# A clamp and a scaling of state ends, moved from GpSimd into VectorE's carry instruction

## The chip, the cores and the metric

The kernel runs on one core of a Trainium2 chip. The metric is the device time in microseconds (us) of one execution, median over the runs. Engines are named as the profile names them: PE is TensorE's matmul, PEld its weight load, DVE is VectorE, ACT is ScalarE, POOL is GpSimd, SP is SyncE. SBUF and PSUM are the two on-chip memories; in this kernel the tiles PM, PAZ and YB lie in PSUM, all other tiles in SBUF.

## What is computed

The reference is a block of a state-space model followed by a mixture of experts. Input x is 8 batches x 1024 steps x 256, inner width 512, state size 16. The part that matters here is the recurrence over time and its clip at every tenth step:

```python
def step(h, inp):
    dA_t, dB_t, x_t, C_t, t = inp
    h = h * dA_t + dB_t * x_t[:, :, None]
    nrm = jnp.sqrt(jnp.sum(h * h, axis=(1, 2), keepdims=True))
    fac = jnp.minimum(20.0 / (nrm + 1e-08), 1.0)
    h = jnp.where(t % 10 == 0, h * fac, h)
    y = jnp.einsum('bdn,bn->bd', h, C_t) + D_param * x_t
    return (h, y)
```

So the states run freely for ten steps, then the whole state of a batch (512 x 16 numbers) is scaled by one factor of at most 1. Behind it come the gate, the output projection, a residual and a layer norm, then a router that takes the best 2 of 8 experts with a capacity, the two expert matmuls, and a second layer norm.

## The kernel before, in words

**Two phases.** `ssm_phase` does the recurrence and its surroundings, `moe_phase` the experts. The change touches only the first, which takes the first 33 or so of the 40 slices of the span. It is a software pipeline over 52 blocks of 20 steps (index i); each block has 16 slots s, the same for each engine. A slot belongs to one batch and one chunk: a block is four quarters (r = s // 4, q = 4 i + r), each the chunk of 10 steps for 4 of the 8 batches, and u = s % 4 is the batch in it. Each engine has its own program with the same two loops, and the order of its work is written out by hand: what stands under which s runs in that order, and semaphores (`wait_ge`, `then_inc`) join the engines.

**The recurrence on VectorE.** For each slot a multiply (`mult`, L579) writes the inputs dB x for 64 rows x 10 steps into PSUM, and a scan (`scan`, L610) runs 64 rows x 11 columns (704 elements per partition), of which column 0 of each row holds the state that is carried in: the decay there is 0, so the scan starts each row from it. The scan writes H, of which three buffers exist (q % 3). Column 10 of each row is the end state. For every two slots one `carry` (L584 to L596) puts the carried states, 2 batches x 64 rows, into column 0 of the scan's input: for q of 2 and more it copies them from the tile CAR. So there are two carries in each q, at u = 0 and u = 2, 412 in all beside four memsets for the first two q. Within two slots VectorE's order is mult(u), carry(u), mult(u + 1), at u = 2 a sum of the norm (L617), the product U = dt x (L566) in two of the 16 slots, scan(u), and then scan(u + 1); at u = 0 the gated output of an earlier q (L631) stands between the two scans. Four further instructions of the block stand between scans and carries: XC (L647, s = 6, ahead of the carry), VV (L697, s = 13), the statistics of a layer norm (L656, s = 14, ahead of the carry; L665 behind it), SG (L705, s = 15) with LGS (L714).

**The clip.** ScalarE squares the end states of q - 1 (L398, one instruction of 256 elements, rows 11 elements apart), TensorE sums them over the partitions (L862), VectorE over the rest (L617, into SN). GpSimd, at u = 2 of q (p = q - 1), raises the sum to the power of -0.5 (L755), multiplies by 1.25 and limits to 1 (L757), and multiplies the end states of p by this factor into CAR (L760), for which it first waits until the carries of p + 1 have read CAR's earlier contents. Carry(q + 1) reads CAR a quarter later: the clip's factor applies to the states that enter chunk p + 2, which is the same batches' next chunk.

**GpSimd's other work.** In every slot it multiplies the ten columns of H by C (L775, 640 elements, in place, "HC" below), which waits for the scan of the slot; TensorE then sums over the 16 states (L820). Besides, per block: L726 (s = 8), L730 (s = 10), L737 and L743 (s = 14), L750 (s = 1), L780 to L786 (s = 3), L793 and L797 (s = 7), in the order in which they stand in the code.

Of the kernel before, what the change touches and what calls it, by code (L numbers as in the profile page):

```python
# [8 lines left out]
ALU = mybir.AluOpType  # L9
ACT = mybir.ActivationFunctionType  # L10
# [12 lines left out]
def ok(j):  # L23
    return 0 <= j < NB
# [77 lines left out]
def ssm_phase(nc, d, YA, X2d, LGd, Bd, Cd, RB, IOE):  # L102
    ctx = ExitStack()
    with ctx:
        def sb(name, shape, dt=F32):
            return ctx.enter_context(nc.sbuf_tensor(name, shape, dt))

        def sem(name):
            return ctx.enter_context(nc.semaphore(name))

        DA = sb("DA", [128, 4, 8, 4, 16, 11])
        H = sb("H", [128, 3, 4, CH])
# [38 lines left out]
        SQ = sb("SQ", [128, 4, 64])  # L151
        SN = sb("SN", [128, 2, 4])
        HALF = sb("HALF", [128, 4])
        FC = sb("FC", [128, 2, 4])
        CAR = sb("CAR", [128, 4, 64])
        PM = ctx.enter_context(nc.psum_tensor("PM", [128, 2048], F32))

        PAZ = ctx.enter_context(nc.psum_tensor("PAZ", [128, 1024], F32))
# [15 lines left out]
        s_bcs, s_ln, s_dth, s_tg, s_z64, s_da, s_x2t, s_hsq = (  # L174
            sem("bcs"), sem("sp"), sem("dth"), sem("tg"), sem("z64"), sem("da"), sem("x2t"), sem("hsq"))

        s_halo, s_sgh, s_dx, s_dxh, s_hc, s_slot = sem("halo"), sem("sgh"), sem("dx"), sem("dxh"), sem("hc"), sem("slot")
        s_min, s_dt, s_xn, s_pow, s_fac, s_car = (
            sem("min"), sem("dt"), sem("xn"), sem("pow"), sem("fac"), sem("car"))
        s_ve, s_sd, s_x2 = sem("ve"), sem("sd"), sem("x2")  # L180

        s_br, s_ssum, s_cv, s_gt, s_dtp = sem("br"), sem("ssum"), sem("cv"), sem("gt"), sem("dtp")
# [2 lines left out]
        s_xc, s_u, s_sg, s_m1, s_ca, s_scan, s_red = (  # L185
            sem("xc"), sem("u"), sem("sg"), sem("m1"), sem("ca"), sem("scan"), sem("red"))
# [19 lines left out]
        def cols(c):  # L206
            return 11 if c < NC - 1 else 1 + (L - 1) % 10
# [5 lines left out]

        def decays(c, g):
            return DA[:, c % 4, 4 * g:4 * g + 4].rearrange("p b a n t -> p b (a n t)")[:, :, 0:64 * cols(c)]

        def U(c):
            return PM[:, 320 * (c % 2):320 * (c % 2) + 320].rearrange("p (a b t) -> p a b t", a=4, b=8)
# [142 lines left out]
        def scalar_program(eng):  # L361
# [11 lines left out]
            def exp_a(j, n):  # L373

                c = 2 * j + n // 2
                v = decays(c, n % 2).rearrange("p b (a t) -> p b a t", t=cols(c))[:, :, :, 1:cols(c)]
                eng.activation(v, v, ACT.Exp, scale=16.0).then_inc(s_da, 1)  # L377
# [12 lines left out]
            for i in range(-4, NB + 3):  # L390
                for s in range(16):
                    q = 4 * i + s // 4
                    if s % 4 == 0 and 1 <= q <= NQ - 2:

                        eng.wait_ge(s_scan, 4 * q)
                        if q >= 2:
                            eng.wait_ge(s_nrm, q - 1)
                        eng.activation(SQ[:], H[:, (q - 1) % 3].rearrange(  # L398
                            "p u (a t) -> p u a t", t=11)[:, :, :, 10], ACT.Square).then_inc(s_hsq, 1)
                    if s == 0 and ok(i + 3):  # L400

                        j = i + 3
# [91 lines left out]
                    if s == 14 and ok(i + 1):  # L494
                        j = i + 1
                        eng.wait_ge(s_gt, 2 * (j + 1))
                        if ok(i + 2):
                            eng.wait_ge(s_xc, j + 2)
                        eng.activation(TB[:].rearrange("p (m a) b t -> p m (a b t)", m=2), BOTH, ACT.Tanh,
                                       scale=0.5).then_inc(s_tg, 1)  # L500
                    if ok(i + 1):
                        j = i + 1
                        c0 = (2 * j) % 4
                        for n in range(DUE[s], DUE[s + 1]):
                            a, m = n // 16, n % 16
                            if n == 0:
# [10 lines left out]
                                scale=AS[:, a, m:m + 1]).then_inc(s_z64, 1)  # L517
# [9 lines left out]
        def vector_program(eng):  # L527
# [56 lines left out]
            def carry(q, u):  # L584

                k = cols(q // 2)
                o = PM[:, 640:640 + 2 * CH].rearrange("p (u n) -> p u n", u=2)[:, :, 0:64 * k].rearrange(
                    "p u (a t) -> p u a t", t=k)[:, :, :, 0]
                if 4 * q + u >= 2:
                    eng.wait_ge(s_scan, 4 * q + u)  # L590
                if q < 2:
                    eng.memset(o, 0.0).then_inc(s_ca, 1)
                else:
                    if u == 0:
                        eng.wait_ge(s_car, q - 1)
                    eng.tensor_copy(o, CAR[:, u:u + 2]).then_inc(s_ca, 1)  # L596

            def scan(q, u):
                eng.wait_ge(s_m1, 4 * q + u + 1)
                eng.wait_ge(s_ca, 2 * q + u // 2 + 1)  # L600
                c, g = q // 2, q % 2
                if u == 0:
                    if q >= 2:
                        eng.wait_ge(s_da, q - 1)
                    if c == NC - 1:
                        eng.wait_ge(s_slot, 1)
                    if q >= 3:
                        eng.wait_ge(s_ys, 3 * (q - 2))
                n = 64 * cols(c)
                eng.tensor_tensor_scan(H[:, q % 3, u, 0:n], decays(c, g)[:, u], DBX(u)[:, 0:n], 0.0, ALU.mult,  # L610
                                       ALU.add).then_inc(s_scan, 1)
# [22 lines left out]
            for i in range(-4, NB + 3):  # L634
                live = ok(i)
                for s in range(16):
                    r, u = s // 4, s % 4
                    q = 4 * i + r
# [18 lines left out]
                    if live and u % 2 == 0:  # L657
                        carry(q, u)
                        mult(q, u + 1)
# [56 lines left out]
        def gpsimd_program(eng):  # L716
            eng.wait_ge(s_pre, PRE_CV)
            for i in range(-4, NB + 3):
                live = ok(i)
                for s in range(16):  # L720
                    r, u = s // 4, s % 4
                    q = 4 * i + r
# [28 lines left out]
                    if u == 2 and 1 <= q <= NQ - 2:  # L751

                        p = q - 1
                        eng.wait_ge(s_red, p + 1)
                        eng.tensor_tensor(FC[:, p % 2], SN[:, p % 2], HALF[:], ALU.pow).then_inc(s_pow, 1)  # L755
                        eng.wait_ge(s_pow, p + 1)
                        eng.tensor_scalar(FC[:, p % 2], FC[:, p % 2], 1.25, 1.0, ALU.mult, ALU.min).then_inc(s_fac, 1)  # L757
                        eng.wait_ge(s_fac, p + 1)
                        eng.wait_ge(s_ca, 2 * (p + 2))
                        eng.tensor_tensor(CAR[:], H[:, p % 3].rearrange("p u (a t) -> p u a t", t=11)[:, :, :, 10],  # L760
                                          FC[:, p % 2].unsqueeze(2).to_broadcast([128, 4, 64]),
                                          ALU.mult).then_inc(s_car, 1)
                    if i == NB - 2 and s == 0:

                        k = cols(NC - 1)
# [177 lines left out]
        with nc.Block() as block:  # L943
            @block.sync
            def _(eng):
                sync_program(eng)

            @block.scalar
            def _(eng):
                scalar_program(eng)  # L950

            @block.vector
            def _(eng):
                vector_program(eng)

            @block.gpsimd
            def _(eng):
                gpsimd_program(eng)

            @block.tensor  # L960
            def _(eng):
                tensor_program(eng)
# [423 lines left out]
def build(nc, d, out):  # L1386
    YA = nc.dram_tensor("YA", [B * LP, DM], F32, kind="Internal").ap()
    X2d = nc.dram_tensor("X2d", [B * LP, DM], F32, kind="Internal").ap()
    LGd = nc.dram_tensor("LGd", [128, 8 * B, E], F32, kind="Internal").ap()
    Bd = nc.dram_tensor("Bd", [NC, 2, NS, 40], F32, kind="Internal").ap()  # L1390
    Cd = nc.dram_tensor("Cd", [NC, 2, NS, 40], F32, kind="Internal").ap()
    with ExitStack() as ctx:
        RB = ctx.enter_context(nc.sbuf_tensor("RB", [128, 4096], F32))
        IOE = ctx.enter_context(nc.sbuf_tensor("IOE", [128, 8], F32))
        ssm_phase(nc, d, YA, X2d, LGd, Bd, Cd, RB[:], IOE[:])
        moe_phase(nc, d, YA, X2d, LGd, out, RB[:])
# [43 lines left out]
```

## Time and profile before

| what | value |
|---|---|
| time, median of 3 runs | 2773.16 us (2772.2 to 2776.47) |
| profiled execution, its span | 2772.7 us (no other time is given for it) |
| busy share of the span | PE 94%, PEld 86%, DVE 86%, ACT 81%, POOL 77% |
| DVE in the 40 slices, tenths | 2999999999999999999999999999999997221124 |
| POOL in the 40 slices, tenths | 0789888898888988989889889898898883434314 |
| granted TensorE clock in the slices | 9899999999999999999999999999999987999996 |
| span on core 0, mean granted clock | 2772.7 us, 0.975 |

A slice is 69.3 us. Each digit is the share of the slice in which the engine was busy, in tenths, where 9 is 90% or more. The recurrence fills slices 2 to 33; the experts follow.

In the rows below, times are us from the start of the span unless marked ns. In a timeline the first number is the start, the second the duration of the record. Records of VectorE follow each other closer than their durations say (the next starts some 0.08 us before the last one's end), so the time that an instruction takes of the engine is read from one start to the next. "x2" means that two instructions in a row are merged into one line.

### The profile page before, as it was taken

What the parts mean: (1) busy time and instruction counts of PE and PEld (TensorE: products, weight loads), DVE (VectorE), ACT (ScalarE), POOL (GpSimd) and SP (SyncE); (2) the same over time, 40 slices, a digit from 0 to 9 for tenths busy, and PEclk for the clock granted to TensorE, in tenths of its full rate; (3) what the DMA queues carried; (4) which work ended last, traced back from release to release, by engine and by line L of the source; (5) the groups of instructions that cost most, each with busy time, mean ns of one, the idle gap of its engine ahead of it and who ended that gap; (6) DMA issues with size and microseconds to landing.
All of it is one profiled execution on the core that took longest, in us unless ns stands there. A gap on an engine that the chain in (4) does not pass through costs nothing. (4 is left out here: it accounts for less than half of the span.)

```text
span 2772.7 us, 50775 instructions
## 1 busy us (share of the span) xinstructions
PE 2593.0 (94%) x16812; PEld 2388.8 (86%) x16812; DVE 2382.4 (86%) x3391; ACT 2245.1 (81%) x5074; POOL 2134.4 (77%) x2237
## 2 busy tenths in 40 slices
PE   5899999999999999999999999999999986899992
PEld 4899999999999999999999999999999975677762
DVE  2999999999999999999999999999999997221124
ACT  5999999999999999999999999999999962111113
POOL 0789888898898988989889889898898883434314
PEclk9899999999999999999999999999999987999996
DMA  1222222222222222222222222222222222234227
GB/s 61 70 78 78 79 80 78 78 78 81 77 78 75 80 79 78 78 78 82 78 78 78 81 78 78 76 78 80 78 78 78 75 78 93 48 93 105 61 48 254
DMA packets 145746, 225.65 MB, mean 81 GB/s; under 512 B 37836, under 2 KB 84684, under 8 KB 144332
## 3 DMA queue, kind: packets, MB, share of 16 engines
q1 hardware_dynamic: 123044, 188.95, 22.4%
q0 software_dynamic: 9216, 12.59, 2.6%
q10 hardware_dynamic: 13224, 20.86, 2.2%
q8 instruction: 134, 2.20, 0.3%
q14 instruction: 128, 1.05, 0.1%
HBM read 189.27 MB, written 33.05 MB: 80 GB/s over the span
## 5 line engine op out<-in xcount | busy, mean ns | idle before, releaser
L775 POOL TENSOR_TENSOR H<-H,CB 128x640 f32<-128x640 f32 (+1 forms) x832 | 1216.2, 1476 | 157.1 <-DVE H L610 154.9
L610 DVE TENSOR_TENSOR_SCAN H<-DA,PM 128x704 f32<-128x704 f32 (+1 forms) x832 | 1309.4, 1594 | 0.0
L514 ACT ACTIVATE DA<-DT,SM 128x160 f32<-128x160 f32 (+1 forms) x3328 | 1106.8, 421 | 1.6 <-POOL DT L737 0.3
L820 PE MATMUL YB<-H,ID 128*128 128x160 f32 (+1 forms) x6656 | 1043.9, 309 | 0.2 <-POOL H L775 0.2
L820 PEld LDWEIGHTS YB<-H,ID 128*128 128x128 f32 x6656 | 982.3, 191 | 16.4 <-issue 11.2
L579 DVE TENSOR_TENSOR PM<-PM,BB 128x640 f32<-128x640 f32 (+1 forms) x832 | 673.1, 809 | 0.0
L377 ACT ACTIVATE DA<-DA 128x2560 f32<-128x2560 f32 (+1 forms) x206 | 477.7, 2319 | 1.7
L755 POOL TENSOR_TENSOR FC<-SN,HALF 128x4 f32<-128x4 f32 x206 | 232.8, 1130 | 40.8 <-DVE SN L617 36.8
L826 PE MATMUL PAZ<-XN,RB 128*128 128x160 f32 x1664 | 254.7, 307 | 0.1
L836 PEld LDWEIGHTS PAZ<-XB,CD 128*128 128x128 f32 x1664 | 237.5, 188 | 16.8
L845 PE MATMUL PAZ<-XC,RB 128*128 128x160 f32 x1664 | 244.4, 300 | 3.3 <-DVE XC L647 3.3
L1285 POOL DMA_INDIRECT YA<-YS,IG x48 | 75.1, 1566 | 219.8 <-ACT YS L1116 208.2
L836 PE MATMUL PAZ<-XB,CD 128*128 128x160 f32 x1664 | 243.1, 297 | 0.0
L826 PEld LDWEIGHTS PAZ<-XN,RB 128*128 128x128 f32 x1664 | 237.9, 195 | 0.7 <-ACT CS L467 0.3
L845 PEld LDWEIGHTS PAZ<-XC,RB 128*128 128x128 f32 x1664 | 231.1, 190 | 6.4 <-DVE XC L647 4.0
L921 PE MATMUL PAZ<-WO,Z 128*80 128x256 f32 x832 | 189.1, 380 | 0.0
L862 PE MATMUL YB<-SQ,MEAN 128*128 128x128 f32 x824 | 131.3, 282 | 43.0 <-ACT SQ L398 43.0
L760 POOL TENSOR_TENSOR CAR<-H,FC 128x256 f32<-128x256 f32 x206 | 155.4, 754 | 17.3
L921 PEld LDWEIGHTS PAZ<-WO,Z 128*80 128x80 f32 x832 | 125.3, 151 | 49.4 <-issue 0.7
L1359 PE MATMUL PE<-W,HT 128*128 128x256 f32 x768 | 167.2, 379 | 0.8 <-issue 0.8
L1348 PE MATMUL PE<-XTE,W 128*128 128x384 f32 x512 | 167.3, 488 | 0.0
L1359 PEld LDWEIGHTS PE<-W,HT 128*128 128x128 f32 x768 | 145.3, 190 | 20.8 <-issue 1.3
(157 smaller groups left out, 2779.7 us busy)
## 6 DMA issues: line engine op xcount, KB each, us to landing
BB<-Bd SPq DMA_DIRECT2D x208, 320.0 KB, 3.4
CB<-Cd SPq DMA_DIRECT2D x208, 320.0 KB, 3.2
W<-in_w ACTq DMA_DIRECT2D x16, 1024.0 KB, 7.9
XT<-in_xT SPq DMA_DIRECT2D x52, 160.0 KB, 2.2
XR<-in_xp SPq DMA_DIRECT2D x208, 40.0 KB
X2d<-VV SPq DMA_DIRECT2D x208, 40.0 KB
YA<-VV SPq DMA_DIRECT2D x208, 40.0 KB
HI<-YA SPq DMA_DIRECT2D x6, 1024.0 KB, 9.9
```

The source lines that it names most:

```text
L377: eng.activation(v, v, ACT.Exp, scale=16.0).then_inc(s_da, 1)
L514: eng.activation(DA[:, c0 + k0:c0 + k1, :, a, m, 1:11].rearrange("p c b t -> p b c t"), DT[:, j % 2, a].rearrange("p b (c t) -> p b c t", ...
L579: eng.tensor_tensor(DBX(u)[:, 0:64 * k].rearrange("p (a n t) -> p a n t", a=4, n=16)[:, :, :, 1:k], U(c)[:, :, 4 * g + u, 0:k - 1].unsquee ...
L610: eng.tensor_tensor_scan(H[:, q % 3, u, 0:n], decays(c, g)[:, u], DBX(u)[:, 0:n], 0.0, ALU.mult, ALU.add).then_inc(s_scan, 1)
L755: eng.tensor_tensor(FC[:, p % 2], SN[:, p % 2], HALF[:], ALU.pow).then_inc(s_pow, 1)
L775: eng.tensor_tensor(h, h, cb, ALU.mult).then_inc(s_hc, 1)
L820: mm = eng.matmul(yv, ID[:], hv[:, :, :, n, 0:w], start=False, stop=n == 15)
L826: mm = eng.matmul(p[:, 160 * a:160 * a + 160], WIN[:, k, c0 + 128 * a:c0 + 128 * a + 128], XN[:, j % 2, k], start=k == 0, stop=k == 1)
L836: mm = eng.matmul(p[:, 160 * a:160 * a + 160].rearrange("p (b t) -> p b t", b=8), CD[:, k, 2 * m + a], XB[:, 2 * m + a, :, k:k + 20], star ...
L845: mm = eng.matmul(p[:, 160 * a:160 * a + 160], WDT[:, k, c:c + 128], XC[:, j % 2, k].rearrange("p b t -> p (b t)"), start=k == 0, stop=k == 3)
L921: mm = eng.matmul(PZ[0:80, 256 * g:256 * g + 256], zf[:, a, 80 * g:80 * g + 80], WO[:, a, :], start=a == 0, stop=a == 3)
L1359: t = eng.matmul(bank(n)[:, 256 * h:256 * h + 256], HT[:, m, 128 * (2 * c + h):128 * (2 * c + h) + 128], W2[:, e % 2, m, :], start=m == 0, ...
```

## The change

The tile CAR and the semaphores `s_fac` and `s_car` go. GpSimd keeps only the power. The factor 1.25 moves into ScalarE's square, which now takes 0.8 h, so that the power yields 1.25 divided by the norm measure. The limit to 1 and the multiplication by the end states are done by VectorE's carry, which was a copy and is now one `scalar_tensor_tensor`: it takes the factor from FC (one number per partition and batch, read with step 0 over 64 rows), the minimum with 1, and multiplies by the end states, read directly from H with a step of 11 elements. It waits for the power (`s_pow`) where it waited for CAR. GpSimd's power waits until the carries of p, which read the FC buffer before, are done.

```diff
-        CAR = sb("CAR", [128, 4, 64])
...
+        def ends(q):
+            return H[:, q % 3].rearrange("p u (a t) -> p u a t", t=11)[:, :, :, 10]
...
-                        eng.activation(SQ[:], H[:, (q - 1) % 3].rearrange(
-                            "p u (a t) -> p u a t", t=11)[:, :, :, 10], ACT.Square).then_inc(s_hsq, 1)
+                        eng.activation(SQ[:], ends(q - 1), ACT.Square, scale=0.8).then_inc(s_hsq, 1)
...
                     if u == 0:
-                        eng.wait_ge(s_car, q - 1)
-                    eng.tensor_copy(o, CAR[:, u:u + 2]).then_inc(s_ca, 1)
+                        eng.wait_ge(s_pow, q - 1)
+                    eng.scalar_tensor_tensor(
+                        o, FC[:, q % 2, u:u + 2].unsqueeze(2).to_broadcast([128, 2, 64]), 1.0, ends(q - 2)[:, u:u + 2],
+                        ALU.min, ALU.mult).then_inc(s_ca, 1)
...
                         eng.wait_ge(s_red, p + 1)
+                        if p >= 2:
+                            eng.wait_ge(s_ca, 2 * (p + 1))
                         eng.tensor_tensor(FC[:, p % 2], SN[:, p % 2], HALF[:], ALU.pow).then_inc(s_pow, 1)
-                        eng.wait_ge(s_pow, p + 1)
-                        eng.tensor_scalar(FC[:, p % 2], FC[:, p % 2], 1.25, 1.0, ALU.mult, ALU.min).then_inc(s_fac, 1)
-                        eng.wait_ge(s_fac, p + 1)
-                        eng.wait_ge(s_ca, 2 * (p + 2))
-                        eng.tensor_tensor(CAR[:], H[:, p % 3].rearrange("p u (a t) -> p u a t", t=11)[:, :, :, 10],
-                                          FC[:, p % 2].unsqueeze(2).to_broadcast([128, 4, 64]),
-                                          ALU.mult).then_inc(s_car, 1)
```

## Rows read from the trace of the kernel before

**Rows 1.** Windows by stretch: us and instructions of each engine, clock, DMA share, GB/s

```profile
1000.00:1500.00 500.00, 491.28 (x3400) 466.89 (x3400) 500.00 (x679) 480.00 (x1065) 442.11 (x464) 1.00 0.27 78
...
102.00:144.00 42.00, 38.52 (x249) 37.26 (x248) 40.25 (x52) 38.00 (x83) 34.91 (x35) 0.92 0.22 67
```

**Rows 2.** VectorE's groups by form, whole span: busy us, mean ns, idle before

```profile
L596 DVE COPY PM<-CAR 128x128 f32<-128x128 f32 x412 | 115.3, 280 | 1.6 <-POOL CAR L760 1.6
...
L566 DVE TENSOR_TENSOR PM<-DT,XC 128x320 f32<-128x320 f32 x104 | 51.8, 498 | 0.0
...
L1225 DVE TENSOR_TENSOR YS<-PE,B 128x512 f32<-128x512 f32 x24 | 16.6, 691 | 147.4 <-PE PE L1359 147.4
...
L549 DVE MEMSET DA<- 128x1536 f32 x1 | 1.3, 1338 | 1.4 <-issue 1.4
...
L86 DVE TENSOR_TENSOR RB<-RB 128x448 f32<-128x448 f32 x2 | 1.5, 752 | 0.1
...
L1153 DVE TENSOR_TENSOR POS<-PE,CI 128x512 f32<-128x512 f32 x1 | 1.0, 1016 | 0.0
```

**Rows 3.** GpSimd's groups by form, whole span

```profile
L775 POOL TENSOR_TENSOR H<-H,CB 128x640 f32<-128x640 f32 x824 | 1210.5, 1483 | 154.1 <-DVE H L610 152.0
L755 POOL TENSOR_TENSOR FC<-SN,HALF 128x4 f32<-128x4 f32 x206 | 232.8, 1130 | 40.8 <-DVE SN L617 36.8
L760 POOL TENSOR_TENSOR CAR<-H,FC 128x256 f32<-128x256 f32 x206 | 155.4, 754 | 17.3
...
L757 POOL TENSOR_SCALAR FC<-FC 128x4 f32<-128x4 f32 x206 | 47.9, 232 | 18.5
```

**Rows 4.** Timeline of VectorE, 1000 to 1045 us: start, us, instruction

```profile
1004.44 0.80 DVE L579 TENSOR_TENSOR PM<-PM,BB 128x640 f32<-128x640 f32 x1
1005.16 0.28 DVE L596 COPY PM<-CAR 128x128 f32<-128x128 f32 x1
1005.35 0.82 DVE L579 TENSOR_TENSOR PM<-PM,BB 128x640 f32<-128x640 f32 x1
...
1007.82 1.60 DVE L610 TENSOR_TENSOR_SCAN H<-DA,PM 128x704 f32<-128x704 f32 x1
1009.35 0.66 DVE L697 SCALAR_TENSOR_TENSOR VV<-XR,PAZ 80x512 f32<-80x512 f32 x1
...
1011.32 0.27 DVE L596 COPY PM<-CAR 128x128 f32<-128x128 f32 x1
...
1031.51 0.80 DVE L579 TENSOR_TENSOR PM<-PM,BB 128x640 f32<-128x640 f32 x1
...
1032.95 0.28 DVE L596 COPY PM<-CAR 128x128 f32<-128x128 f32 x1
```

**Rows 5.** Timeline of GpSimd, 1000 to 1045 us

```profile
1009.51 1.49 POOL L775 TENSOR_TENSOR H<-H,CB 128x640 f32<-128x640 f32 x1 [0.20 <-DVE H L610]
1011.08 0.72 POOL L737 TENSOR_SCALAR DT<-TA 128x640 f32<-128x640 f32 x1
```

**Rows 6.** Timeline of VectorE, 2225 to 2310 us

```profile
2234.31 0.97 DVE L566 TENSOR_TENSOR PM<-DT,XC 128x320 f32<-128x320 f32 x1
2235.20 3.12 DVE L610 TENSOR_TENSOR_SCAN H<-DA,PM 128x704 f32<-128x704 f32 x2
...
2307.39 0.88 DVE L86 TENSOR_TENSOR RB<-RB 128x448 f32<-128x448 f32 x1
```

**Rows 7.** Timeline of GpSimd, 2225 to 2310 us

```profile
2232.02 2.91 POOL L775 TENSOR_TENSOR H<-H,CB 128x640 f32<-128x640 f32 x2
2234.89 1.25 POOL L755 TENSOR_TENSOR FC<-SN,HALF 128x4 f32<-128x4 f32 x1
...
2306.70 1.09 POOL L786 TENSOR_SCALAR VV<-VV,NME,SD 80x256 f32<-80x256 f32 x2
```

**Rows 8.** ScalarE's groups by form, whole span

```profile
L398 ACT ACTIVATE SQ<-H 128x256 f32<-128x256 f32 x206 | 134.1, 651 | 8.7 <-DVE H L610 8.6
...
L408 ACT ACTIVATE TB<-XT 128x320 f32<-128x320 f32 x52 | 23.7, 456 | 0.0
```

More of the change, by code:

```diff
@@ L177, in ssm_phase @@
         s_halo, s_sgh, s_dx, s_dxh, s_hc, s_slot = sem("halo"), sem("sgh"), sem("dx"), sem("dxh"), sem("hc"), sem("slot")
-        s_min, s_dt, s_xn, s_pow, s_fac, s_car = (
-            sem("min"), sem("dt"), sem("xn"), sem("pow"), sem("fac"), sem("car"))
+        s_min, s_dt, s_xn, s_pow = sem("min"), sem("dt"), sem("xn"), sem("pow")
         s_ve, s_sd, s_x2 = sem("ve"), sem("sd"), sem("x2")
```

## The prediction

> **What bounds the kernel now.** I read the profile's page first, for the phases: its slices show VectorE at 9 tenths through the recurrence. Then the windows inside that phase, then the groups by form of the three engines that the change touches, and last VectorE's and GpSimd's timelines side by side. In the window of 500 us VectorE is busy for all 500.00, TensorE 491.28, ScalarE 480.00, GpSimd 442.11 [rows 1]. VectorE has no gap, so each nanosecond added to one of its instructions here lengthens the loop, and each one taken from GpSimd is worth nothing unless VectorE waits for GpSimd. It does so once in the whole trace, for 1.6 us ahead of a carry [rows 2]; GpSimd waits for VectorE's scans, for 152 us in all [rows 3].
>
> **What the change removes.** GpSimd loses 206 instructions of 232 ns and 206 of 754 ns [rows 3], some 203 us of busy time and a little idle time between them. It lies beside VectorE's work and shortens nothing. The 1.6 us may go: the power was ready far earlier than CAR. I count -1.6 us. ScalarE's square gets a constant scale instead of none: the same instruction of 651 ns [rows 8], on an engine with 4% of slack; nothing. Should it cost 50 ns, four a block are 0.2 us, and the slack of a block is over 1 us. GpSimd's new wait, for the carries of p, is always met: by then VectorE has gone past the carries of p + 1. The tile and the two semaphores cost no time. No DMA is moved, and no queue of SP or GpSimd is passed.
>
> **What it adds.** VectorE's 412 copies become 412 instructions with two inputs, FC and H, both in SBUF. A copy takes 0.19 us from its start to the next one's, 1005.16 to 1005.35 [rows 4]. Three prices are to be found.
>
> First, the pure work. The copy of 128 elements is 280 ns, a two-input operation of 512 elements with one input in PSUM is 691 ns [rows 2]; the line through both is 1.07 ns per element on 143 ns. At 320 elements it gives 485; L566, which has both inputs in SBUF, has 498 on average, and without its one long instance (970) it is 493 [rows 2, 6]. So a second input costs nothing by itself, and I take 0.
>
> Second, the step of 11 elements in H. No VectorE instruction before reads SBUF so. The nearest is L1153, which reads CI with a step of 64 elements (and PSUM with the same): 1016 ns against 691 for L1225 at the same 512 elements [rows 2], 0.63 ns per element, so 0.081 us for 128 and 33.4 us for 412. The low end is 0: L549 writes every eleventh element and takes 1338 ns for 1536, 0.87 ns each [rows 2]. A gain is excluded, since the same number of elements is read. The high end is ScalarE, which reads these very end states: 651 ns for 256 against 456 for 320 contiguous ones [rows 8]; with 64 elements less counted at 1.07 ns that is 263 ns too much, 1.03 each, 0.132 us for 128 and 54 us for 412. I take 33.4, from the row of the same engine.
>
> Third, and largest, GpSimd. Two places show what VectorE does when both inputs are in SBUF and GpSimd is in the middle of an instruction. L566 at 2234.31 lasts 0.97 us in place of 0.49 [rows 6, 2], while GpSimd's two HC run to 2232.02 + 2.91 = 2234.93 [rows 7]: it was lengthened by 0.48, which is the 0.62 us to GpSimd's end less 0.14. The following scan starts at 2235.20, so the engine lost it in full. L86 at 2307.39 lasts 0.88, where its two instances sum to 1.5 us, so the other had 0.62 [rows 6, 2]; GpSimd's L786 runs to 2306.70 + 1.09 = 2307.79 [rows 7]: 0.40 to its end, 0.26 too long, again 0.14 less. The other 103 L566 stand right behind the norm sum, where GpSimd waits for that sum, and meet nothing. Scans, mults and the copy have at most one input in SBUF and keep their durations beside HC all along.
>
> The Trainium skill's page "SBUF — State Buffer", section "Who interferes with whom", has the rule: a VectorE instruction with two SBUF inputs and a GpSimd instruction that reads SBUF share a read interface, and whichever comes second is blocked until the first is done. By that rule, the trace agrees. The Trainium skill's page "Advanced Engine Details and Errata", section "SBUF Cachelines", says that accesses which each go to another 16-byte line pay a penalty, but gives no price; by it the zero end of the second price falls away, while the memset's row shows no penalty.
>
> Where does GpSimd stand when a carry asks? Call T the start of VectorE's first instruction behind the second scan of a pair (1009.35). GpSimd's HC of that scan starts at 1009.51 = T + 0.16 and ends 1.49 later, at T + 1.65 [rows 4, 5]. The carry asks one mult behind T: 1005.16 - 1004.44 = 0.72 [rows 4]. So it finds HC running and waits 1.65 - 0.72 - 0.14 = 0.79 us. With two instructions gone GpSimd is less loaded than now, so each such HC starts when its scan ends; its block of extra work falls behind HC and is over before the next pair. Of the eight carries of a block five are like this (s = 2, 4, 8, 10, 12): 3.95 us. At s = 6 XC stands ahead, and the carry asks at T + 1.44, 1031.51 to 1032.95 [rows 4]: 0.07. At s = 0 SG and LGS stand ahead: 0. At s = 14 VV and the statistics stand ahead, and the carry at 1011.32 meets DT, which runs 1011.08 to 1011.80 [rows 4, 5]: 0.34. Sum 4.36 us a block; 412 / 8 = 51.5 blocks make 224.5 us. Low end: waits of 0, if FC's step-0 read did not count as an SBUF input. High end: no 0.14 to be deducted, six times 0.14 x 51.5 = 43 more.
>
> **The sum.** 2772.7 + 224.5 + 33.4 - 1.6 = 3029.0 us for the profiled execution; the median of the runs shown is 0.5 above its span, within their spread, so I forecast 3029. TensorE, at 98% of the loop now, falls to some 88% and ScalarE to 86%; neither hides any of this, for VectorE is late in every slot. Late next is GpSimd's HC, by the same amount, then TensorE's sums.
>
> **Rivals.**
> *A, the engines slide past each other.* If HC and carries meet at random, the mean wait is the sum of squared durations over twice the block: 16 x 1.483² + 4 x 1.13² is 40, over 94 gives 0.43, less 0.14 x 28/47 is 0.35 us. 412 x 0.35 = 144, so 2772.7 + 144 + 33 - 2 = 2948. For it: GpSimd's extra work moves HC; against it: HC is tied to the scan and the carry too. 11%.
> *B, not slower.* VectorE gets its operands at once, because a factor of two numbers a partition is hardly a stream, and the strided read is free as the strided memset was. Place: each carry; it decides if carries stay at 0.2 us from start to start. Then 1.6 us are gained, and 0.48 at the one long L566: 2770.6, less than 0.1% below. Against it: L566 and L86. 3%, with 1 more for a gain over 0.2%, for which no row has a source.
> *C, only the stride costs:* 2772.7 + 33.4 - 1.6 = 2804.5. 4%.
> *D, GpSimd goes twice.* If its next ready instruction enters ahead of the waiting carry, slots 4, 8 and 10 wait for L780, L793 or L730 too; at the 0.72 us of L737 [rows 5] for each that is 2.2 us a block, 111 in all: 3140. Against it: L755 was ready at 2234.89 and was itself stretched, to 1.25 us [rows 7], so VectorE came first. 3%.
> *E, TensorE's clock.* The granted clock is 1.00 at 98% busy and 0.92 in the stretch where TensorE was busy for 38.52 of 42 us [rows 1]. A block is now some 42.6 us (32 slices of 69.3 over 52 blocks), 42 of them matmul at full clock; at 0.92 these are 46 of 47.6, so it decides only below 0.88. At 0.84 a block would be 50, 120 us more: 3150. 2%.
> That the change does not do what it says is no case: the diff leaves no copy.
>
> **How the numbers follow.** The forecast has 76%; its own range goes from no stride price (2995) to no deduction and ScalarE's price (2772.7 + 224.5 + 43 + 54 = 3094). The range reaches down to A: 2945 to 3098; left out are B, C, D, E and tails. A measurement of this kernel can tell about 0.2% from no change. Faster 0.01, same 0.03, slower 0.96.
>
> **What would show it.** L596's successor with a mean near 1.0 us at slots 2, 4, 8, 10 and 12, each ending some 0.35 us behind an HC's end, and near 0.36 at slots 0 and 6. The shortest of them show the stride's price over 280 ns. VectorE still busy for all of each window, mults and scans unchanged, GpSimd's waits for the scan grown. I am wrong on the mechanism if long carries end without GpSimd's end nearby, on the size if HC starts later than T + 0.16, and on all if carries stay at 0.28.

## The result, and the profile after

The changed kernel takes 3027.63 us (median of 4 runs, 3026.03 to 3028.15) against 2773.52 us for the kernel before (4 runs): a ratio of 1.0913, 95% interval 1.0898 to 1.0929. It is 9% slower. The span of the profiled execution grew from 2772.7 to 3025.7 us, by 253.0.

From the page of the kernel after, its busy times and the slices of two engines and of the granted clock:

```profile
PE 2656.8 (88%) x16812; PEld 2420.4 (80%) x16812; DVE 2636.3 (87%) x3391; ACT 2267.9 (75%) x5074; POOL 1987.5 (66%) x1825
...
DVE  2999999999999999999999999999999998522214
...
POOL 1677777777777777777777777777777774533324
PEclk8999999999999999999999999999999988799996
```

A slice is 75.6 us now. VectorE is at 9 tenths all through the recurrence, as before, and GpSimd has fallen from 8 or 9 to 7. The window inside the loop (PE, PEld, DVE, ACT, POOL, clock, DMA share, GB/s):

```profile
1000.00:1500.00 500.00, 449.48 (x3056) 420.11 (x3055) 500.00 (x609) 435.18 (x968) 368.85 (x335) 1.00 0.24 70
```

Beside [rows 1] VectorE is the only engine that did not get idle: still 500.00 us of 500, with 609 instructions in place of 679. TensorE fell from 491 to 449, ScalarE from 480 to 435. VectorE sets the pace as before, and needs more time for the same work. The groups by form show on which instruction, VectorE's first:

```profile
L596 DVE SCALAR_TENSOR_TENSOR PM<-FC,H 128x128 f32<-128x128 f32 x412 | 368.0, 893 | 0.0
...
L566 DVE TENSOR_TENSOR PM<-DT,XC 128x320 f32<-128x320 f32 x104 | 51.3, 493 | 0.0
```

The carry went from 115.3 us to 368.0 for the same 412 instructions [rows 2]: +252.7 us of the 253.0 that the span grew. Its mean of 893 ns hides two kinds, as the timeline will show. L566 is unchanged but for the one long instance of before. GpSimd's groups:

```profile
L772 POOL TENSOR_TENSOR H<-H,CB 128x640 f32<-128x640 f32 x824 | 1220.1, 1481 | 473.8 <-DVE H L612 452.4 <-ACT DA L514 9.9
L759 POOL TENSOR_TENSOR FC<-SN,HALF 128x4 f32<-128x4 f32 x206 | 229.0, 1112 | 155.6 <-DVE SN L619 155.6
...
L790 POOL TENSOR_TENSOR DX<-XC,SM 128x640 f32<-128x640 f32 x52 | 73.4, 1411 | 0.0
L739 POOL TENSOR_SCALAR DT<-TA 128x640 f32<-128x640 f32 x52 | 61.2, 1177 | 17.5 <-ACT TA L489 12.9
```

Idle time ahead of HC, nearly all of it spent waiting for the scan, grew from 154.1 to 473.8 us [rows 3], and ahead of the power from 40.8 to 155.6: what GpSimd was relieved of, and more, is idle time now. L790 (L793 before, 1256 ns there) and L739 (L737 before, 725 ns there) have become longer, though their code is the same: GpSimd is held up too.

VectorE's timeline with three kinds of carry (start, us):

```profile
999.85 0.81 DVE L579 TENSOR_TENSOR PM<-PM,BB 128x640 f32<-128x640 f32 x1
1000.56 1.18 DVE L596 SCALAR_TENSOR_TENSOR PM<-FC,H 128x128 f32<-128x128 f32 x1
1001.65 0.82 DVE L579 TENSOR_TENSOR PM<-PM,BB 128x640 f32<-128x640 f32 x1
...
1019.20 0.37 DVE L596 SCALAR_TENSOR_TENSOR PM<-FC,H 128x128 f32<-128x128 f32 x1
1019.48 0.82 DVE L579 TENSOR_TENSOR PM<-PM,BB 128x640 f32<-128x640 f32 x1
...
1025.11 0.38 DVE L596 SCALAR_TENSOR_TENSOR PM<-FC,H 128x128 f32<-128x128 f32 x1
1025.40 0.82 DVE L579 TENSOR_TENSOR PM<-PM,BB 128x640 f32<-128x640 f32 x1
...
1042.85 0.45 DVE L596 SCALAR_TENSOR_TENSOR PM<-FC,H 128x128 f32<-128x128 f32 x1
```

and GpSimd's in the same window:

```profile
1000.01 1.48 POOL L772 TENSOR_TENSOR H<-H,CB 128x640 f32<-128x640 f32 x1
1001.44 1.41 POOL L790 TENSOR_TENSOR DX<-XC,SM 128x640 f32<-128x640 f32 x1
...
1018.96 1.20 POOL L739 TENSOR_SCALAR DT<-TA 128x640 f32<-128x640 f32 x1
```

The carry of s = 8 asks for its operands (its record starts) at 1000.56, 0.55 after HC's record began. HC ends at 1001.49, the carry at 1001.74, and the next mult starts at 1001.65: 1.09 us from start to start, where the copy took 0.19 [rows 4]. At s = 14 (1019.20) and s = 0 (1025.11) it lasts 0.37 and 0.38, 0.28 and 0.29 from start to start: this is the carry alone. At s = 6 (1042.85) it catches the last 0.2 us of an HC, which stands beside it in GpSimd's timeline (1041.57, 1.49), and lasts 0.45. One block has five carries of 1.17 to 1.19 and these three, 7.1 us in all. At s = 14 it is GpSimd that loses time: DT, 0.72 us before [rows 5], lasts 1.20.

### The profile page after: what moved, and what is told of

The parts are those of the page before. It is cut to its first block and busy times, and to the rows that moved or that the text cites. A ratio compares the mean times of both kernels' runs of the same rounds, so it can differ in the third digit from the quotient of the medians.

```text
span 3025.7 us, 50361 instructions
## 1 busy us (share of the span) xinstructions
PE 2656.8 (88%) x16812; PEld 2420.4 (80%) x16812; DVE 2636.3 (87%) x3391; ACT 2267.9 (75%) x5074; POOL 1987.5 (66%) x1825
## 5 line engine op out<-in xcount | busy, mean ns | idle before, releaser
L817 PE MATMUL YB<-H,ID 128*128 128x160 f32 (+1 forms) x6656 | 1059.2, 312 | 0.0
L817 PEld LDWEIGHTS YB<-H,ID 128*128 128x128 f32 x6656 | 998.8, 194 | 15.9 <-issue 11.2
L823 PE MATMUL PAZ<-XN,RB 128*128 128x160 f32 x1664 | 276.7, 317 | 127.7 <-DVE VV L699 127.6
L596 DVE SCALAR_TENSOR_TENSOR PM<-FC,H 128x128 f32<-128x128 f32 x412 | 368.0, 893 | 0.0
L823 PEld LDWEIGHTS PAZ<-XN,RB 128*128 128x128 f32 x1664 | 246.4, 200 | 140.4 <-DVE VV L699 139.7
L759 POOL TENSOR_TENSOR FC<-SN,HALF 128x4 f32<-128x4 f32 x206 | 229.0, 1112 | 155.6 <-DVE SN L619 155.6
L399 ACT ACTIVATE SQ<-H 128x256 f32<-128x256 f32 x206 | 136.6, 663 | 181.7 <-DVE H L612 181.5
```

The source lines that it names most:

```text
L596: eng.scalar_tensor_tensor(o, FC[:, q % 2, u:u + 2].unsqueeze(2).to_broadcast([128, 2, 64]), 1.0, ends(q - 2)[:, u:u + 2], ALU.min, ALU.mu ...
L817: mm = eng.matmul(yv, ID[:], hv[:, :, :, n, 0:w], start=False, stop=n == 15)
L823: mm = eng.matmul(p[:, 160 * a:160 * a + 160], WIN[:, k, c0 + 128 * a:c0 + 128 * a + 128], XN[:, j % 2, k], start=k == 0, stop=k == 1)
```

## The experiments

Each comparison is with runs of the kernel before on the same chip: 2775.83 us for x1 to x4, 2774.81 us for x5 to x8.

Three terms are used all through. "Port theory" stands for the third price of the prediction: a VectorE instruction with two tensors in SBUF waits until the GpSimd instruction that is running has ended. A "plain" carry is one with only a mult ahead of it, at s = 2, 4, 8, 10 and 12. T is the start of VectorE's first instruction behind the second scan of a pair.

**x2_step: the step alone.**

```diff
-                    eng.tensor_copy(o, CAR[:, u:u + 2]).then_inc(s_ca, 1)
+                    eng.tensor_copy(o, H[:, (q - 2) % 3].rearrange(
+                        "p u (a t) -> p u a t", t=11)[:, u:u + 2, :, 10]).then_inc(s_ca, 1)
```

> The kernel before, but the carry's copy reads the end states directly from H with the step of 11 elements; GpSimd still writes CAR, which nobody reads, so the clip is left out of what is carried. One SBUF input. Port theory: no waits, each copy 0.09 us longer than 0.28, 412 x 0.09 = 37 us: about 2810 us. Rival, the step is what costs: near 3026 us. Rival, the 0.09 us is something else than the step: 2773 us.

Measured: 2814.25 us, 38.4 more, ratio 1.0138 (1.0109 to 1.0168). VectorE's copy by form:

```profile
L596 DVE COPY PM<-H 128x128 f32<-128x128 f32 x412 | 156.5, 380 | 1.2 <-POOL CAR L761 1.2
```

With one input in SBUF it waits for nobody; the step of 11 elements makes 380 ns of 280, 0.78 ns for each of 128 elements. 412 x 0.10 = 41.2 us, and the time grew by 38.4. This measures the second price apart from everything else.

**x1_packed: two inputs without the step.** To the kernel after it adds CAR again, as an unscaled, packed copy of the end states:

```diff
+                        eng.wait_ge(s_car, q - 1)
...
-                        o, FC[:, q % 2, u:u + 2].unsqueeze(2).to_broadcast([128, 2, 64]), 1.0, ends(q - 2)[:, u:u + 2],
+                        o, FC[:, q % 2, u:u + 2].unsqueeze(2).to_broadcast([128, 2, 64]), 1.0, CAR[:, u:u + 2],
...
+                        eng.wait_ge(s_ca, 2 * (p + 2))
+                        eng.tensor_copy(CAR[:], ends(p)).then_inc(s_car, 1)
```

> The kernel after, but GpSimd first copies the end states, unscaled, into the packed tile CAR, and the carry reads FC and CAR: two SBUF inputs as before, no step of 11 elements. Port theory (the carry waits for GpSimd's running instruction): unhindered carries fall to some 0.28 us, the hindered ones stay near 1.1; 412 x 0.09 = 37 us less than after, some 10 to 15 back because GpSimd's copy delays its products: about 3000 us. Rival, the step is what costs: back to about 2775 us.

Measured: 3022.4 us, ratio 1.0888 (1.0856 to 1.092). The carry by form, two of its instances (s = 14 and s = 0), and what GpSimd ran ahead of and beside the second one:

```profile
L598 DVE SCALAR_TENSOR_TENSOR PM<-FC,CAR 128x128 f32<-128x128 f32 x412 | 365.3, 887 | 0.4 <-POOL CAR L763 0.4
```

```profile
1018.62 0.27 DVE L598 SCALAR_TENSOR_TENSOR PM<-FC,CAR 128x128 f32<-128x128 f32 x1
...
1024.45 1.04 DVE L598 SCALAR_TENSOR_TENSOR PM<-FC,CAR 128x128 f32<-128x128 f32 x1
```

```profile
1021.79 0.64 POOL L763 COPY CAR<-H 128x256 f32<-128x256 f32 x1
1022.39 2.93 POOL L776 TENSOR_TENSOR H<-H,CB 128x640 f32<-128x640 f32 x2
```

Unhindered it lasts 0.27: no price for the second input, and the 0.10 of the step is gone. But the time hardly fell, and one slot explains it. GpSimd's copy of 0.64 us delays the two HCs that follow it. At s = 0 the carry, which in the kernel after met only the last 0.1 us of an HC and lasted 0.38, now finds 0.87 us of it left, and lasts 1.04. Over the whole trace the median at s = 0 is 1.04 us, and from start to start such a carry takes 0.69 more than in the kernel after with the step deducted: 35 us for 51 of them. The plain carries wait as long as before (1.08 us in place of 1.18, the step's 0.10 less). Step saved, waits gained: x1 is 246.6 us above its kernel before, the changed kernel 254.1 above its own, so some 34 of the 41 us came back, where I had put 10 to 15. One rival goes with this run and x2: that the carry waits because it reads H, the tile that HC works on. Here it waits and does not read H; in x2 the copy reads H beside HC and does not wait.

**x3_half_hc: GpSimd's instruction made shorter.**

```diff
-                        h = H[:, q % 3, u, 0:64 * k].rearrange("p (a n t) -> p a n t", a=4, n=16)[:, :, :, 0:n]
-                        cb = CB[:, q % 2, :, u, 0:n].unsqueeze(1).to_broadcast([128, 4, 16, n])
+                        h = H[:, q % 3, u, 0:64 * k].rearrange("p (a n t) -> p a n t", a=4, n=16)[:, :, :, 0:n // 2]
+                        cb = CB[:, q % 2, :, u, 0:n // 2].unsqueeze(1).to_broadcast([128, 4, 16, n // 2])
```

> The kernel after, with GpSimd's product HC over 5 of the 10 columns (the other half of the product with C is left out). HC should last some 0.85 us, so it ends at T + 1.0 and a plain carry that asks at T + 0.72 waits 0.15 in place of 0.8. Port theory: 2773 + 37 (step) + 5 x 0.15 x 51.5 = 39, about 2850 us. Rival, the carry's length has nothing to do with how long GpSimd's instruction runs: 3026 us.

Measured: 2878.0 us, ratio 1.0368 (1.0338 to 1.0398). GpSimd's group, VectorE around a plain carry, and the HC beside it:

```profile
L772 POOL TENSOR_TENSOR H<-H,CB 128x320 f32<-128x320 f32 x824 | 755.2, 917 | 757.9 <-DVE H L612 751.7 <-ACT DA L514 0.8
```

```profile
1000.68 0.81 DVE L579 TENSOR_TENSOR PM<-PM,BB 128x640 f32<-128x640 f32 x1
1001.39 0.62 DVE L596 SCALAR_TENSOR_TENSOR PM<-FC,H 128x128 f32<-128x128 f32 x1
1001.93 0.82 DVE L579 TENSOR_TENSOR PM<-PM,BB 128x640 f32<-128x640 f32 x1
```

```profile
1000.84 0.92 POOL L772 TENSOR_TENSOR H<-H,CB 128x320 f32<-128x320 f32 x1 [0.60 <-DVE H L612]
```

The carry asks 0.55 us after HC's start, as in the kernel after, but HC ends 0.56 us earlier (0.92 in place of 1.48), and the carry is 0.56 us shorter (0.62 in place of 1.18). In both kernels its end lies 0.25 us behind HC's. HC was longer than the 0.85 that I had assumed; with five waits of 0.25, 64 us, and the step's 41, the sum is 2775.8 + 105 = 2881. VectorE's own instruction is the same in both kernels, so the length of what GpSimd runs sets the carry's.

**x4_late: the same carry, asked later.**

```diff
-                        carry(q, u)
                         mult(q, u + 1)
+                        carry(q, u)
```

> The kernel after, with the carry moved behind the second mult of its pair: it asks 0.73 us later, at T + 1.44, when HC has 0.2 us to run. Port theory: waits of 0.07 us in place of 0.8 at the five plain slots, so 2773 + 37 + some 8 x 0.05 x 51.5 = 20, about 2830 us. Rival, the two-input instruction is slow beside any GpSimd work: unchanged, 3026 us.

Measured: 2900.67 us, ratio 1.045 (1.0419 to 1.048). VectorE and GpSimd:

```profile
1004.93 0.45 DVE L596 SCALAR_TENSOR_TENSOR PM<-FC,H 128x128 f32<-128x128 f32 x1
...
1009.98 0.45 DVE L596 SCALAR_TENSOR_TENSOR PM<-FC,H 128x128 f32<-128x128 f32 x1
1010.52 1.62 DVE L612 TENSOR_TENSOR_SCAN H<-DA,PM 128x704 f32<-128x704 f32 x1
...
1016.50 0.98 DVE L596 SCALAR_TENSOR_TENSOR PM<-FC,H 128x128 f32<-128x128 f32 x1
```

```profile
1015.54 0.74 POOL L739 TENSOR_SCALAR DT<-TA 128x640 f32<-128x640 f32 x1
1016.36 0.86 POOL L745 TENSOR_TENSOR XN<-XT,RST 128x320 f32<-128x320 f32 x1
```

At the plain slots the prediction of 0.07 us holds: 0.45 in place of 1.18, with no other change than 0.72 us of position. The total is 71 us above the 2830 that I expected: two costs were not in my sum. The scan needs the carry's result, and with nothing between them it starts 0.54 us behind the carry (1009.98 to 1010.52) where 0.36 is the carry's own: 0.18 us, four times a block at u = 0 (at u = 2 the norm sum stands between). And at s = 14 the carry now falls on XN, which began 0.14 us before it at 1016.36: 0.98. Together 0.72 + 0.60 = 1.3 us a block, 68 us, and with those 2830 becomes 2898, against 2900.67 measured.

**x5_later: later still**, behind the norm sum or the gated output, right ahead of the scan:

```diff
-                        carry(q, u)
                         mult(q, u + 1)
...
+                    if u == 0 and 0 <= q - 3 < NQ:
+                        z_out(q - 3)
+                    if live and u % 2 == 0:
+                        carry(q, u)
                     if live:
                         scan(q, u)
-                    if u == 0 and 0 <= q - 3 < NQ:
-                        z_out(q - 3)
```

> The kernel after, with the carry moved right ahead of the scan, behind the second mult and behind the norm sum or the gated output where these stand in the pair: it asks at T + 1.63 or later, when HC has at most 0.02 us to run. Port theory: no waits left, only the step's price, 2773 + 412 x 0.09 = 2810 us. Rival, the second input has a price of its own beyond the waits: above 2830 us.

Measured: 2961.32 us, ratio 1.0675 (1.0657 to 1.0693): a miss by 150 us.

```profile
1000.98 0.38 DVE L596 SCALAR_TENSOR_TENSOR PM<-FC,H 128x128 f32<-128x128 f32 x1
1001.45 3.13 DVE L612 TENSOR_TENSOR_SCAN H<-DA,PM 128x704 f32<-128x704 f32 x2
...
1023.36 1.43 DVE L596 SCALAR_TENSOR_TENSOR PM<-FC,H 128x128 f32<-128x128 f32 x1
1024.88 3.13 DVE L612 TENSOR_TENSOR_SCAN H<-DA,PM 128x704 f32<-128x704 f32 x2
```

```profile
1023.27 1.26 POOL L791 TENSOR_TENSOR DX<-XC,SM 128x640 f32<-128x640 f32 x1
```

In the excerpt seven of eight carries are as short as they can be, 0.38. But each is now followed at once by the scan that needs it, 0.47 from start to start in place of 0.29: 0.18 x 8 = 1.4 us a block, 74 us. And at s = 8 the carry at 1023.36 comes 0.09 us behind the start of GpSimd's L791, the next instruction in its row, and waits for that one: 1.43. That is 1.05 us a block, 54 us. The step adds 41. The sum is 169 of the 187 us. The excerpt does not show a third meeting: in 32 of 52 blocks the carry at s = 14 catches the end of XN, and lasts 0.64 where it lasts 0.38 in the others, 9 us in all:

```profile
994.70 0.64 DVE L596 SCALAR_TENSOR_TENSOR PM<-FC,H 128x128 f32<-128x128 f32 x1
```

```profile
994.21 0.87 POOL L746 TENSOR_TENSOR XN<-XT,RST 128x320 f32<-128x320 f32 x1
```

Added up over the trace, the 412 carries take 261.1 us from start to start, the 412 copies before 79.1: 182 of the 187 us lie at the carries. The time alone would have spoken for the rival (above 2830); the records speak for the port theory, since the carries that meet nothing cost only the step. My placing was wrong.

**x6_pointer: the factor as a scalar per partition.** GpSimd limits the four factors; the carry is two instructions, each with one tensor input:

```diff
-                        eng.wait_ge(s_pow, q - 1)
+                        eng.wait_ge(s_fac, q - 1)
-                    eng.scalar_tensor_tensor(
-                        o, FC[:, q % 2, u:u + 2].unsqueeze(2).to_broadcast([128, 2, 64]), 1.0, ends(q - 2)[:, u:u + 2],
-                        ALU.min, ALU.mult).then_inc(s_ca, 1)
+                    eng.tensor_scalar(o[:, 0], ends(q - 2)[:, u], FC[:, q % 2, u:u + 1], None, ALU.mult)
+                    eng.tensor_scalar(o[:, 1], ends(q - 2)[:, u + 1], FC[:, q % 2, u + 1:u + 2], None,
+                                      ALU.mult).then_inc(s_ca, 1)
...
+                        eng.wait_ge(s_pow, p + 1)
+                        eng.tensor_scalar(FC[:, p % 2], FC[:, p % 2], 1.0, 1.0, ALU.mult, ALU.min).then_inc(s_fac, 1)
```

> The kernel after, with the limit to 1 done by GpSimd on the 4 factors and the carry as two instructions of 64 elements that take the factor as a scalar per partition and only the end states as a tensor from SBUF. If only two tensor inputs meet the port: no waits, but a second start, 2 x 0.165 in place of 0.19 us, 412 x 0.14 = 58 us: about 2831 us. Rival, a scalar from SBUF counts as an input too: as slow as after or slower, 3026 to 3080 us.

Measured: 2889.16 us, ratio 1.0416 (1.0398 to 1.0433). The two groups, and one pair in the timeline:

```profile
L597 DVE TENSOR_SCALAR PM<-H,FC 128x64 f32<-128x64 f32 x412 | 134.0, 325 | 0.0
L596 DVE TENSOR_SCALAR PM<-H,FC 128x64 f32<-128x64 f32 x412 | 133.9, 325 | 0.1
```

```profile
1004.16 0.33 DVE L596 TENSOR_SCALAR PM<-H,FC 128x64 f32<-128x64 f32 x1
1004.40 0.33 DVE L597 TENSOR_SCALAR PM<-H,FC 128x64 f32<-128x64 f32 x1
1004.63 0.82 DVE L579 TENSOR_TENSOR PM<-PM,BB 128x640 f32<-128x640 f32 x1
```

The operands from SBUF are the same, end states and factor, but only one is a tensor; all 412 pairs are alike (a minimum of 304 ns and a maximum of 351) and none waits, though HC had begun 0.55 us before the carry in the plain slots here too. So it is the second tensor input that meets GpSimd. Each takes 0.23 to 0.24 from start to start, not 0.165, so the pair costs 0.47 against 0.19: 412 x 0.28 = 115 us, which is the whole difference. Still 138 us better than the one instruction it replaces.

**x7_relief: GpSimd's relief alone.** In the kernel before:

```diff
-                        eng.tensor_scalar(FC[:, p % 2], FC[:, p % 2], 1.25, 1.0, ALU.mult, ALU.min).then_inc(s_fac, 1)
-                        eng.wait_ge(s_fac, p + 1)
...
-                        eng.tensor_tensor(CAR[:], H[:, p % 3].rearrange("p u (a t) -> p u a t", t=11)[:, :, :, 10],
-                                          FC[:, p % 2].unsqueeze(2).to_broadcast([128, 4, 64]),
-                                          ALU.mult).then_inc(s_car, 1)
+                        eng.tensor_copy(CAR[:], H[:, p % 3].rearrange("p u (a t) -> p u a t", t=11)[:, :, :, 10]).then_inc(s_car, 1)
```

> The kernel before with GpSimd's relief alone: the instruction that limits the factor is gone, and CAR is a copy of the end states with one input (the clip's scaling is left out of what is carried); VectorE's carry is untouched. Theory, VectorE sets the pace and GpSimd's time is covered: 2773 us, less by at most 2. Rival, GpSimd's load is part of what sets the pace: 2760 us or less.

Measured: 2774.27 us (10 runs) against 2774.81 (13), ratio 0.9999 (0.999 to 1.0009).

```profile
1000.00:1500.00 500.00, 491.25 (x3405) 467.38 (x3404) 500.00 (x677) 480.00 (x1061) 427.10 (x420) 1.00 0.27 78
```

GpSimd is busy for 427 us in place of 442, VectorE for all 500 as before, and the time is the same. This takes away only some 70 us of GpSimd's 203 (48 for L757, 24 for the shorter copy), so it shows the rule for that part; that the rest was covered as well rests on VectorE's 500 of 500.

**x8_early: the carry first.** Behind the scan, ahead of both mults:

```diff
                     if live and u % 2 == 0:
+                        carry(q, u)
                         mult(q, u)
...
-                        carry(q, u)
                         mult(q, u + 1)
```

> The kernel after, with the carry as the first instruction behind the scan: it asks at T or just after, before HC takes the port at T + 0.16 or later, so it goes first and HC follows. It must wait for the scan just ahead of it on its own engine, whose price I put at 0.15 us. Port theory with who asks first goes first: 2773 + 412 x (0.09 + 0.15) = 2872 us. Rival, GpSimd's HC gets in first: the carry waits all of HC, 412 x 1.4 more, over 3250 us.

Measured: 2986.56 us, ratio 1.0764 (1.0746 to 1.0782).

```profile
1000.73 0.39 DVE L596 SCALAR_TENSOR_TENSOR PM<-FC,H 128x128 f32<-128x128 f32 x1
...
1018.78 0.39 DVE L596 SCALAR_TENSOR_TENSOR PM<-FC,H 128x128 f32<-128x128 f32 x1
...
1023.93 2.12 DVE L596 SCALAR_TENSOR_TENSOR PM<-FC,H 128x128 f32<-128x128 f32 x1
```

```profile
1000.31 2.15 POOL L772 TENSOR_TENSOR H<-H,CB 128x640 f32<-128x640 f32 x1 [0.19 <-DVE H L612]
...
1022.89 2.92 POOL L772 TENSOR_TENSOR H<-H,CB 128x640 f32<-128x640 f32 x2
```

In six of eight slots it goes as expected: the carry at 1018.78 lasts 0.39, and HCs are stretched (HC's mean rose from 1.48 to 1.59). At 1000.73 the carry asks 0.42 us behind the start of HC's record and still goes first; HC lasts 2.15. But where GpSimd runs late, the carry loses more than any before. At 1023.93 GpSimd has two HCs in a row, to 1025.81; the carry asks 0.4 us before the first ends, and lasts until 1026.05, behind the second. GpSimd went twice, and it did so in 49 of the 51 blocks with this slot (s = 6). At s = 0 the carry asks 0.6 us into the second HC of a pair and lasts 1.10 (median). Neither of my two forecasts, 2872 or over 3250, gave this mixture; the trace adds up to it: from start to start the 412 carries take 171 us more than the copies before, and the 310 that stand right behind a scan start 0.12 us later than a mult does there, 36 us, together 207 of the 212.

## Why the prediction was right

The forecast was 3029, the result 3027.6. This is closer than its steps were: errors of 5 to 18 us with different signs nearly cancel, and that is luck. On the span the forecast was 3029.0 and the measured value 3025.7, so 253.0 us were added where I had put 256.3; the median lies 1.9 us above the span in place of my 0.5. The steps one by one:

*VectorE sets the pace, GpSimd's relief is worth nothing.* Right; the windows after and x7 show it. The 1.6 us wait for CAR went, as said.

*The second input has no price of its own.* Right: 0.27 us unhindered in x1, against 0.28 for the copy.

*The step.* Right in kind, too small: 0.081 us taken from L1153, 0.10 measured in x2, so 41 us in place of 33.4. The zero that the memset's row gave as the low end was wrong (it writes with the step, and the carry reads with it), and the other end, ScalarE's 0.132, too high. By the Trainium skill's page "Advanced Engine Details and Errata", section "SBUF Cachelines", accesses that each go to another line cost more; the trace agrees, with the 0.78 ns per element of x2.

*The wait for GpSimd's running instruction.* Right, and the bulk. At the five plain slots the carry was to wait for 0.79 us; it waits 1.18 - 0.37 = 0.81. The two rows of before that gave "time to GpSimd's end less 0.14" gave it well: 0.93 less 0.12. x3 shows that the wait follows the length of HC, x4 that it follows the carry's position, x6 that it needs a second tensor input. At s = 6 it was 0.08 against 0.07, at s = 0 0.01 against 0. My list of signs did not fit my own sum: 0.36 + 0.79 makes a record of 1.15, not "near 1.0", and an end 0.36 - 0.14 = 0.22 us behind HC's, not 0.35; measured were 1.18 and 0.25. By the Trainium skill's page "SBUF — State Buffer", section "Who interferes with whom", the one that comes second is blocked until the first is done; the trace agrees, with the carry's end 0.25 us behind HC's for two lengths of HC. Which of the two comes second can't be read from the starts of their records, as the next slot shows.

*The slot s = 14* is the term that failed. I had the carry wait 0.34 us for DT, because DT's record had begun before it. The carry waited for nothing, and DT was stretched by 0.48 us, in 49 of 52 blocks. My reading is that the start of a GpSimd record is not yet the start of its hold on what the two share; no run tests this apart. That was 17.5 us too much, against 8 too little for the step and 5 too little for the plain slots. In sum: waits 252.7 - 41.2 = 211.5 us in place of 224.5, step 41.2 in place of 33.4; together 252.7 in place of 257.9.

*The rivals.* B and C fell with the long carries; A with their regularity (in the excerpt all five plain slots agree within 0.02 us; over the whole trace the mean of each of the five lies between 1162 and 1188 ns, and the longest single carry is 1623); E with a granted clock of 1.00, the higher of the two levels, in the window where TensorE was 90% busy. D did not occur in the excerpt, but I had dismissed it on the strength of one row, and x8 shows that GpSimd can go twice. With the carry at another place in the row the sum would have been another.

## What to carry to other kernels

A VectorE instruction with two tensors in SBUF beside a busy GpSimd costs its own time plus what is left of GpSimd's running instruction, and at one place in x8 the next one too; read it from the two timelines, at the point where it will ask, and not from its element count. Fusing a step of an engine with slack into an instruction of the engine that sets the pace wins only what that engine waited for, here 1.6 us: 203 us were taken from an engine with slack, worth nothing, and 253 put on the one without. If it must be fused, a factor given as a scalar per partition, or one of the operands in PSUM, should keep the instruction from waiting for GpSimd (the first was run: no waits, and 4% slower than before; the second is what mults and scans here have, which keep their durations beside HC, and was not tried for the carry).

## What was not expected of the hardware

- Who goes first is not told by the starts of the records. Behind an idle GpSimd, a carry that asks 0.42 us after HC's start goes first (x8), at 0.55 us it waits (after, x3). Behind another GpSimd instruction the carry loses already at 0.09 us (L791 in x5) and 0.14 us (XN in x4), while against DT, with one tensor input, it goes first at 0.24 us (after). The rule behind these five is open.
- A carry that waited for one HC was passed by the next one in x8 (2.12 us), in 49 of 51 blocks at that slot, but never in the excerpt of the kernel after, where at 1001.44 it was L790, next in GpSimd's row, that was stretched; what decides is open too.
- A scan right behind the carry that it needs starts 0.18 us later than the carry's own time would let it (x4, x5), and in x8 a carry right behind a scan 0.12 us later. An instruction between the two hides this, as the mult did in the kernel before.
- Two instructions of 64 elements with a scalar per partition take 0.23 us each from start to start, where the line through larger ones, with the step, gave 0.165.
